# Last FFN's projection and rotation in one stage, its attention by blocks, and expert routing by sorted chunks

## The reference

```python
h = shift_token(x)
q, k, v = split(h @ wqkv)               # heads of 64
q = l2norm(q) * qs; k = l2norm(k) * ksc
q, k = rotary_xpos(q, k)                # q*cos*scale + rotate_half(q)*sin*scale; k the same with 1/scale
bq = q.reshape(b, h, w, 64, d) * 8.0    # a query block sees its own block of keys and the one before
mask = (i < j) | (i > j + 64) | (j == -1)
attn = softmax(where(mask, -max, bq @ bk.T)); o = attn @ bv
x = x + o @ wo                          # then a gated net, and x = x + net
```

## Time and profile before

| what | value |
|---|---|
| median of the runs | 1954.29 us |
| the profiled execution's own time | 1955.33 us |
| its span | 1953.6 us |
| TensorE busy | 1400.2 us (72%) |
| VectorE busy | 1194.9 us (61%) |
| ScalarE busy | 694.5 us (36%) |
| GpSimd busy | 440.2 us (23%) |
| granted TensorE clock, mean | 0.835 |

### The profile page before, as it was taken

The page is one execution under the profiler, slowest core; times in us unless marked ns, Lnnn a source line. Parts: engine busy times, 40 slices in busy tenths (PEclk is TensorE's granted clock), DMA queues, the critical chain, the costliest instruction groups (busy, mean ns, idle before and its releaser), DMA issues. The chain is left out here.

```text
span 1953.6 us, 23816 instructions
## 1 busy us (share of the span) xinstructions
PE 1400.2 (72%) x8378; PEld 1055.8 (54%) x8378; DVE 1194.9 (61%) x2335; ACT 694.5 (36%) x1421; POOL 440.2 (23%) x454
## 2 busy tenths in 40 slices
PE   5888888988686985836719847587268738863785
PEld 3666666666563654714509735465237516732572
DVE  5899999999255664155595464334458277437744
ACT  3465665565132761312302220042033233423341
POOL 2566556565102002101003110000010050005000
PEclk8999899999796996967859868599679867976697
DMA  6101110110101002500014200000100000000000
GB/s 208 34 26 39 40 34 26 40 34 1 56 1 33 1 1 82 163 2 1 13 43 160 83 0 1 1 1 32 55 0 1 1 0 1 1 1 0 1 1 11
DMA packets 31030, 59.85 MB, mean 31 GB/s; under 512 B 6592, under 2 KB 17856, under 8 KB 30656
## 3 DMA queue, kind: packets, MB, share of 16 engines
q1 hardware_dynamic: 29888, 56.09, 8.9%
q0 software_dynamic: 1024, 2.23, 0.5%
HBM read 54.13 MB, written 4.18 MB: 30 GB/s over the span
## 5 line engine op out<-in xcount | busy, mean ns | idle before, releaser
L187 POOL TENSOR_TENSOR rstd<-spread,minus_half 128x4 f32<-128x4 f32 x36 | 36.8, 1023 | 960.5 <-DVE spread L169 960.5
L917 PE MATMUL l0h_scores<-l0h_k_rot,l0h_q_slots 128*128 128x128 f32 (+1 forms) x1024 | 206.9, 349 | 0.0
L917 PEld LDWEIGHTS l0h_scores<-l0h_k_rot,l0h_q_slots 128*128 128x128 f32 x1024 | 169.8, 208 | 13.2
L1134 POOL TENSOR_TENSOR l0h_k_part<-large_weights,l0h_sines 128x512 f32<-128x512 f32 x64 | 83.9, 1311 | 177.1 <-PE l0h_scores L917 129.1
L1008 ACT ACTIVATE l0h_scores<-l0h_scores,l0h_top 128x128 f32<-128x128 f32 (+1 forms) x256 | 100.4, 392 | 27.7 <-DVE l0h_top L1087 27.5
L1081 DVE TENSOR_TENSOR l0h_q_slots<-l0h_q_rot,l0h_chosen 128x1024 f32<-128x1024 f32 x64 | 78.4, 1225 | 6.7
L893 PE MATMUL l0h_projected<-XT,l0h_wq 128*128 128x256 f32 x256 | 70.1, 397 | 15.2 <-ACT large_weights L979 11.9
L1135 POOL TENSOR_TENSOR l0h_k_rot<-large_weights,l0h_cosines 128x512 f32<-128x512 f32 x64 | 80.8, 1263 | 0.0
L907 PE MATMUL l0h_scores<-l0h_key_masks,l0h_query_picks 4*128 4x128 bf16 (+1 forms) x256 | 45.0, 257 | 49.0 <-DVE l0h_probs L1104 49.0
L1087 DVE TENSOR_REDUCE l0h_top<-l0h_scores 128x2 f32<-128x256 f32 (+1 forms) x128 | 65.0, 546 | 6.6 <-PE l0h_scores L917 6.4
L1446 ACT ACTIVATE l0n_probs<-l0n_scores,l0n_top 128x256 f32<-128x256 f32 x128 | 53.8, 482 | 39.0 <-DVE l0n_top L1477 38.9
(11 more groups left out here) (718 smaller groups left out, 3658.7 us busy)
## 6 DMA issues: line engine op xcount, KB each, us to landing
l1e_experts<-in_l_experts SPq DMA_DIRECT2D x16, 768.0 KB, 4.4
l0e_experts<-in_l_experts SPq DMA_DIRECT2D x15, 578.0 KB, 4.5
l0h_chosen<-l0h_chosen_dram SPq DMA_DIRECT2D x64, 128.0 KB, 3.0
small_weights<-in_w_l_ffn SPq DMA_DIRECT2D x1, 4016.0 KB, 12.9
...
```

The costliest lines, as they stand in the source:

```text
L917: mm = nc.tensor.matmul(at[:, slot], q_slots[:, s % 2, slot, part, i * P:(i + 1) * P], k_rot[:, s % 2, part, 0:KEYS[i][1]], start=False, s ...
L1134: nc.gpsimd.tensor_tensor(k_part[:], source, at_batch(sines, s), ALU.mult)
```

## The change

*Routing.* The probabilities are turned once as 128 x 128: a partition then holds one expert's 128 values of one tile, and all 128 chunks are sorted at once by 16 rounds of eight, the chunks of tiles 4 to 7 with their sign changed. SyncE moves the sorted chunks to 16 partitions (eight copies from SBUF to SBUF). VectorE merges: the greater of one falling and one rising list of 128 keeps the 128 greatest, a cascade of maxima and minima sorts them again, until one list is left; its least value is each expert's threshold. Tokens above it and tokens equal to it are marked, and TensorE counts ranks with bf16 matmuls.

```diff
+                nc.tensor.transpose(chunks_ps[:], exps[:].rearrange("p t e -> p (t e)"), k.ident[:])\
...
+                nc.tensor.transpose(least_ps[:], best[:], k.ident[0:E1, 0:E1]).then_inc(least_turned, 1)
...
+                nc.tensor.matmul(ranks_ps[:, 0:T, :], k.above[:], marked[:], start=True, stop=False,
+                                 skip_group_check=True)
...
                 for t in range(T):
-                    mm = nc.tensor.transpose(slot_ps[:, t, :], place[:, t * P:(t + 1) * P], k.ident[0:E1, 0:E1])
-                mm.then_inc(slots_ready, 1)
+                    mm = nc.tensor.matmul(ranks_ps[:, t + 1:, :], k.ones16[:],
+                                          bc(marked[:, t, :].unsqueeze(1), [P, T - t, 2 * E1]), start=False,
+                                          stop=(t == T - 1), skip_group_check=True)
...
-                for _ in range(CAP // 8):
-                    link(v, nc.vector.max(best[:], left[:]))
-                    link(v, nc.vector.match_replace(left[:], best[:], left[:], -1.0))
...
+                link(v, nc.vector.tensor_scalar(left[:], chunks_ps[:], sign[:], None, ALU.mult))
+
+                for r in range(P // 8):
+                    best8 = in_order[:, 8 * r:8 * r + 8]
+                    last = nc.vector.max(best8, left[:])
+                    if 8 * r + 8 < P:
+                        link(v, last)
+                        link(v, nc.vector.match_replace(left[:], best8, left[:], -2.0))
+                last.then_inc(sorted_ready.sem, 1)
...
-                link(v, nc.vector.tensor_tensor(shared[:], shared[:], ups[:], ALU.mult))
-                v.wait_ge(slots_ready, 1)
-                link(v, nc.vector.tensor_copy(slot[:], slot_ps[:]))
+                nc.vector.tensor_tensor(shared[:], shared[:], ups[:], ALU.mult)
+
+                def sort(lists_of, at):
+                    step = P // 2
+                    while step:
+                        of, to = (x.rearrange("e l (g o s) -> e l g o s", o=2, s=step)
+                                  for x in (merged[:, at, 0:lists_of], merged[:, 1 - at, 0:lists_of]))
+                        nc.vector.tensor_tensor(to[:, :, :, 0], of[:, :, :, 0], of[:, :, :, 1], ALU.max)
+                        link(v, nc.vector.tensor_tensor(to[:, :, :, 1], of[:, :, :, 0], of[:, :, :, 1], ALU.min))
+                        at, step = 1 - at, step // 2
+                    return at
+
+                def merge(to, down, up, half):
+                    nc.vector.scalar_tensor_tensor(to[:, 0:half], up[:, 0:half], -1.0, down[:, 0:half], ALU.mult, ALU.max)
+                    link(v, nc.vector.scalar_tensor_tensor(to[:, half:2 * half], down[:, half:2 * half], -1.0,
+                                                           up[:, half:2 * half], ALU.mult, ALU.min))
+
+                v.wait_ge(listed, 16 * T)
+                merge(merged[:, 0], lists[:, 0:4], lists[:, 4:8], 2)
+                at = sort(4, 0)
+                merge(merged[:, 1 - at], merged[:, at, 0:2], merged[:, at, 2:4], 1)
+                at = sort(2, 1 - at)
+                link(v, nc.vector.scalar_tensor_tensor(best[:], merged[:, at, 1, :], -1.0, merged[:, at, 0, :], ALU.mult,
+                                                       ALU.max))
+                link(v, nc.vector.tensor_reduce(least[:], best[:], AX.X, ALU.min))
+                nc.vector.tensor_copy(best[:], bc(least[:], [E1, P])).then_inc(least_ready.sem, 1)
+                v.wait_ge(least_turned, 1)
+                link(v, nc.vector.tensor_copy(sums[:, 0:E1], least_ps[:]))
...
+                nc.vector.tensor_tensor(above[:], exps[:], least_of, ALU.is_gt)
+                link(v, nc.vector.tensor_tensor(equal[:], exps[:], least_of, ALU.is_equal))
+                nc.vector.tensor_copy(marked[:, :, 0:E1], above[:])
+                nc.vector.tensor_copy(marked[:, :, E1:], equal[:]).then_inc(marked_ready, 1)
...
+                link(v, nc.vector.tensor_copy(sums[:], ranks_ps[:, T, :]))
+                total_above = bc(sums[:, 0:E1].unsqueeze(1), full)
+                link(v, nc.vector.tensor_tensor(slot[:], ranks_ps[:, 0:T, E1:], total_above, ALU.add))
+                nc.vector.scalar_tensor_tensor(above[:], ranks_ps[:, 0:T, 0:E1], 1.0, above[:], ALU.add, ALU.mult)
+                link(v, nc.vector.scalar_tensor_tensor(equal[:], slot[:], float(CAP), equal[:], ALU.is_lt, ALU.mult))
+                link(v, nc.vector.scalar_tensor_tensor(slot[:], slot[:], 1.0, equal[:], ALU.add, ALU.mult))
+                link(v, nc.vector.scalar_tensor_tensor(slot[:], slot[:], 1.0, above[:], ALU.subtract, ALU.add))
```

```diff
+            @block.sync
+            def _(sp):
+                full, one = T * HL * (DL + 1), HL * (DL + 1)
+                sp.wait_ge(by_vector.sem, by_vector.base + T // 2)
+                sp.wait_ge(ones_set.sem, ones_set.base + 1)
+                sp.dma_start(late[WINDOW:P, 0:full], flat[0:WINDOW, 0:full]).then_inc(late_ready.sem, 16)
+                sp.dma_start(late[0:WINDOW, one:full], flat[WINDOW:P, 0:full - one]).then_inc(late_ready.sem, 16)
...
+                    part, c = order[n]
+                    if n >= 3:
+                        counted, count = (by_vector, by_vector.base + c) if part == 2 else \
+                            (by_scalar, by_scalar.base + 2 * (c - 1) + part + 1)
+                        pe.wait_ge(counted.sem, count)
...
+                for c in range(T // 2):
+                    for part in range(3):
+                        project(3 * c + part)
+                    if c >= 2:
+                        turn(2 * c - 4)
+                        turn(2 * c - 3)
+                for n in range(T // 2, len(tiles)):
+                    turn(n)
...
+                for c in range(T // 2):
+                    for part in range(2):
+                        act.wait_ge(projected.sem, projected.base + 3 * c + part + 1)
+                        nc.scalar.copy(rows["qk"[part]][:, 2 * c:2 * c + 2], both(areas[:, part, :]))
+                        if c >= 2:
+                            act.wait_ge(by_vector.sem, by_vector.base + c - 1)
+                        nc.scalar.activation(squares(part, c), areas[:, part, :], ACT.Square).then_inc(by_scalar.sem, 1)
+                    if c >= 2:
+                        copy_turned(2 * c - 4)
+                        copy_turned(2 * c - 3)
+                act.wait_ge(clipped.sem, clipped.base + 1)
+                nc.scalar.sqrt(sums[:], sums[:]).then_inc(rooted.sem, 1)
+                for n in range(T // 2, len(tiles)):
+                    copy_turned(n)
...
+                def rotate(n):
+                    x, t = tiles[n]
+                    one = by_head(rows[x][:, t])
+                    v.wait_ge(part_ready.sem, part_ready.base + n + 1)
+                    link(v, nc.vector.tensor_tensor(one, one, bc(tables["cos_" + x][:, t % TB].unsqueeze(1),
+                                                                 [P, HL, DL]), ALU.mult))
+                    nc.vector.tensor_tensor(one, one, by_head(parts[:, t]), ALU.add).then_inc(tile_ready.sem, 1)
...
+                for c in range(T // 2):
+                    for part in range(2):
+                        v.wait_ge(by_scalar.sem, by_scalar.base + 2 * c + part + 1)
+                        last = nc.vector.tensor_reduce(sums[:, part, 2 * c:2 * c + 2].rearrange("p t h -> p (t h)"),
+                                                       squares(part, c).rearrange("p (a d) -> p a d", d=DL), AX.X, ALU.add)
+                    v.wait_ge(projected.sem, projected.base + 3 * c + 3)
+                    last = nc.vector.tensor_copy(values[:, 2 * c:2 * c + 2, :, 0:DL].rearrange("p t h d -> p (t h) d"),
+                                                 areas[:, 2, :].rearrange("p (x d) -> p x d", d=DL))
+                    last.then_inc(by_vector.sem, 1)
+                    if c >= 1:
+                        rotate(2 * c - 2)
+                        rotate(2 * c - 1)
+                v.wait_ge(by_vector.sem, by_vector.base + T // 2)
+                nc.vector.tensor_scalar(sums[:, 0], sums[:, 0], QK_SCALE ** -2, (1e-12 / QK_SCALE) ** 2, ALU.mult, ALU.max)
+                nc.vector.tensor_scalar(sums[:, 1], sums[:, 1], 1e-24, None, ALU.max).then_inc(clipped.sem, 1)
+                v.wait_ge(rooted.sem, rooted.base + 1)
+                link(v, nc.vector.reciprocal(inverse[:], sums[:]))
+                for t in range(T):
+                    one = by_head(rows["k"][:, t])
+                    nc.vector.tensor_tensor(one, one, bc(inverse[:, 1, t].unsqueeze(2), [P, HL, DL]), ALU.mult)\
+                        .then_inc(k_ready.sem, 1)
+                    if t < 2:
+                        rotate(T - 2 + t)
+                for n in range(T, 2 * T):
+                    rotate(n)
...
                 for n, (x, t) in enumerate(tiles):
-
-                    if n >= T:
-                        g.wait_ge(tile_ready.sem, tile_ready.base + n - T + 1)
```

(71 more changed lines are left out.)

297 lines of the change are left out of this document (156 added, 141 removed).

## The result

The changed kernel takes **1873.87 us**, median of 4 runs (1872.72 to 1878.64), beside 1954.36 for the kernel before on the same chip (4 runs, 1953.05 to 1957.53). The ratio is **0.9598, 95% interval 0.9586 to 0.9611**: 80.5 us faster. The forecast was 1882 in a range of 1858 to 1908. The profiled execution took 1872.72 with a span of 1870.9, against a span of 1953.6 before: 82.7 less.

What follows compares the result with a forecast made beforehand. It took VectorE to bound routing and rotation, and TensorE the projection products and attention. Terms of -19.2 (routing), -38 (projection and rotation), -16 (attention) and +1 (masks) gave -72.2, from 1954.3 to 1882 us; range 1858 to 1908.

Steps and rivals of the forecast that it cites:

- Routing, 19.2: Routing from the turn of the probabilities to the slot copy: 32.4 us against 51.6, so 19.2 less.
- The loads: Routing: SyncE's eight SBUF-to-SBUF copies, 0.44 each to issue, with the reader starting 1.6 after the last issue, 4.8 us together.
- the bound of 6 us for strides: Routing merge: strided reads could make the 28 exchange steps cost 6 us more; the range kept 0 to 6.
- Projection and rotation, 38: Projection with rotation: each layer's stage ends at 61.6 us against 80.2, taken as 19 less, 38 for both layers.
- The rival of the lock in full: Rotation: VectorE and GpSimd exclude each other, 44 instructions taking 30.4 us, not 25.0; +15 for both layers, 1897, chance 0.11.
- Attention, 16: Attention over the windows: a unit takes 3.0 us instead of 3.52; 8.0 less a layer, 16 for both.
- the price of the scores: Attention: a unit's 16 score records of 64 x 64 x 128 were priced at 1.03 us.
- the rival with a chance of 0.14: Attention scores: four 64 x 64 parts of TensorE work at once, scores at 0.6 us, 13 less, 1869; chance 0.14.
- TensorE stays the path: Attention: TensorE bounds a unit, ScalarE having 2.0 us beside 2.5 of scores and weighing, and VectorE 1.5.
- That 0.5: Start of attention: the half-clock start costs 0.5 us more a layer, the first two units having twice the score records.
- That 64-column parts don't overlap: Attention rival: half blocks save no TensorE time, weighing and scores 0.87 more each, 52 in all, 1934; chance 0.06.
- That the clock stays low: Projection and attention rival: TensorE stays at 1.2 GHz because waits break its work, 111 us more, 1993; chance 0.04.

## Why the prediction was right, and where it was not

*The sum* of 72.2 stands against 80.5; the sign and the range held. The order of the terms did not: attention was forecast as the smallest of the three (16) and gave the second most (27.3), ahead of routing (17.5). The error is nearly all in this one term. That the total came within 8.5 us of the forecast is in part luck: a unit's scores were priced 0.43 us too high, and a loop of handovers, for which the sum had 0.1 of waiting, takes back 0.31. For routing and projection the mechanism was right as forecast; for attention it was not.

*Routing, 19.2 against 17.5.* The rounds: 0.71 each against 0.68 priced, 0.5 in all. The loads: 5.04 us of issue for eight, 0.63 each, where the earlier trace rows had 0.44 for loads from DRAM; the merge starts 6.2 us after the first issue and not 4.8. That is the term that was mis-sized here: a row of another kind of transfer taken for this one. The merge at even rate (0.41 for 256 values) was right, and the bound of 6 us for strides was not needed. The shared multiply is covered by the loads, as forecast: it ends at 982.3, the merge waits until 986.3.

*Projection and rotation, 38 against 36.9.* The steps end where forecast: the root is called 33.05 us after the stage's start, by the forecast's clock 33.15. The rest is 29.0 against 28.4, with 7.6 of contention against 6.6. The two 1 MB copies of the values are issued at 1560 and hide behind the rotations.
The rival of the lock in full gave 30.4 us for the 44 instructions after the root; they take 25.9 (1564.32 to 1590.2). So neither one rate nor the other: an overlapped VectorE instruction is stretched from 0.69 to 1.1 or 1.2, but not by the whole of GpSimd's, and the cost measured is 7.6 us a layer, not the 12 (30.4 - 18.4) of the rival. Two-input instructions are stretched beside GpSimd's reads; filling with zeros stretches none of them, and reductions keep 1.22 beside GpSimd. "SBUF — State Buffer" of the Trainium skill (SBUF: two separate sides) has an exclusive lock for whole instructions between two-input VectorE instructions and GpSimd's reads. The runs agree with it on who disturbs whom, and not on the size.

*Attention, 16 against 27.3.* The step that failed is the price of the scores, "for lack of a 64 x 64 row, 1.03": it is 0.60. Four parts work at once, the rival with a chance of 0.14, shown by the kernel with two parts (1.08). Its estimate of 0.45 a unit was right, but not all of it arrived: with the other terms near the forecast (turn 0.49 for 0.45, masks 0.31 for 0.4, weighing 1.03) TensorE's own unit is 2.43, and the kernel runs at 2.74. That is the second failed step: ScalarE's "2.0, beside the 2.5 of scores and weighing", from which the forecast concluded that "TensorE stays the path". I compared busy times, and not the loop in which they follow one another: exponents 1.51, their handover and the turn, copy 0.58, and only then the next exponents on the same engine. The exponents were undersized too: four in 1.51 (0.464 each, overlapping) against 4 x 0.335 from the earlier trace rows. Of the 0.78 that a unit gained, 0.52 were forecast; the loop withholds 0.31.
The 11.3 missed can be placed by the starts of the turns. From the third turn on, 13 units took 46.3 us before and 35.6 after: 10.7 less a layer and not 6.8. The tail behind the last turn is 5.2 and 3.4, the 1.7 forecast. From the end of the stage to the third turn it was 13.1 and 12.9, and is 11.6 and 12.1: 1.6 and 0.8 less, where the forecast had 0.5 more. That 0.5 stood for "twice the score records" at the lower clock. But the 16 records take 1.06 us there, and the 8 of before took 1.16, from their start to the next work:

```profile
1592.82 1.13 PE L3279 MATMUL l3f0a_scores<-l3f_k_t,l3f_q_t 64*64 64x128 f32 x16
1593.88 0.60 PE L3271 MATMUL l3f0a_scores<-masker,l3f_far_first 128*128 128x256 bf16 x2
```

```profile
1629.17 1.23 PE L3050 MATMUL l3f_att_scores<-l3f_k_t,l3f_q_t 64*128 64x128 f32 x8
1630.33 0.61 PE L3045 MATMUL l3f_att_scores<-masker,l3f_far_own 128*128 128x256 bf16 x2
```

So this is the failed price of the scores once more. How soon a layer reaches 2.4 GHz differs: in the first 12 us of the second layer the granted clock was 0.55 in the first trace and 0.84 in the later one, and attention took 50.9 and 48.7. The kernel is the same in both. I had no term for that, and what decides it was not tried.
"TensorEngine Tiling (Array Packing)" of the Trainium skill (Tiling Modes) has four independent 64 x 64 parts; the trace agrees, with groups of four records 0.11 us apart and of two where only two parts are used.

*The other rivals.* That 64-column parts don't overlap is refuted by the weighing, 1.03 for 16 records. That the clock stays low is refuted by the windows: 0.88 in the steps, 1.00 from 1601 on. It was 0.50 from the root to the end of the stage, where VectorE is the path and TensorE has slack (busy for 12.1 of 29 us), and 0.52 in the first 8.8 us of attention.

*The signs.* Exchange steps of 0.41 and the clock of 1.00 in attention spoke for the forecast. The sign of being wrong that did appear was that of the score records, 16 in 0.60 us in groups of four 0.11 apart. VectorE was busy for 51.1 of the stage's 62.3 us, eight tenths and not nine.
